# Fused attention kernel: transposes join the score banks, value sums move three groups back, V is loaded whole for the last tile, and the last keys of four heads share a tile

## The reference

```python
scores = jnp.einsum('bthd,bghd->bhtg', Q, K) / np.sqrt(DH)
topv, topi = jax.lax.top_k(scores, K_TOP)            # K_TOP = 32
probs = jax.nn.softmax(topv, axis=-1)
attn = jnp.zeros_like(scores).at[bi, hi, ti, topi].set(probs)
attn_mean = attn.mean(axis=1)                        # over the 4 heads
c_t = jnp.einsum('btg,bgd->btd', attn_mean, V)       # V: 6404 x 128
```

```python
scores = jnp.einsum('bhqd,bhkd->bhqk', q, k) / jnp.sqrt(D)
out = jnp.einsum('bhqk,bhkd->bhqd', jax.nn.softmax(scores, axis=-1), v)
```

## Time and profile before

| | us |
|---|---|
| Median of 3 runs | 2005.47 (2000.84 to 2008.52) |
| The profiled execution | 2001.17, its span 1999.4 |
| First attention, 198 to 862 us of the span | 664 |
| Second attention, 1075 to 1813 | 738 |
| PE, DVE, ACT busy, whole span | 1590.6, 857.4, 1387.5 |

### The profile page before, as it was taken

How to read it: one execution, slowest core, us unless ns; L and a number is a source line. 1 busy time by engine, 2 the same in 40 slices (tenths; PEclk the granted TensorE clock), 3 DMA queues, 4 the chain that set the end, 5 groups by cost and what they waited for, 6 DMA issues and landing times. The chain is left out here.

```text
span 1999.4 us, 22599 instructions
## 1 busy us (share of the span) xinstructions
PE 1590.6 (80%) x8229; PEld 609.5 (30%) x8229; DVE 857.4 (43%) x2286; ACT 1387.5 (69%) x1382; POOL 177.6 (9%) x153
## 2 busy tenths in 40 slices
PE   4357978888788788356464999999999999995996
PEld 3236334445444455333220111111111111113332
DVE  5734699999899898836320000000000000003223
ACT  3471678778778787410224999999999999992432
POOL 2743021111111111100000000000000000000000
PEclk8566989999999999678666999999999999997998
DMA  2122086796786876767002000610070000003000
GB/s 86 51 92 97 11 163 150 165 209 144 172 193 136 196 166 157 167 110 113 21 12 37 1 1 1 56 14 1 7 64 1 1 1 1 1 1 91 0 0 11
DMA packets 91348, 145.08 MB, mean 73 GB/s; under 512 B 46704, under 2 KB 59465, under 8 KB 90433
## 3 DMA queue, kind: packets, MB, share of 16 engines
q0 software_dynamic: 13472, 75.53, 18.9%
q1 hardware_dynamic: 77328, 67.19, 15.7%
q10 hardware_dynamic: 432, 0.85, 0.1%
HBM read 54.15 MB, written 13.99 MB: 34 GB/s over the span
## 5 line engine op out<-in xcount | busy, mean ns | idle before, releaser
L1735 ACT ACTIVATE ex<-ps 128x1536 f32<-128x1536 f32 x544 | 731.2, 1496 | 1.2 <-PE ps L1694 1.0
L1707 PE MATMUL ps<-ex,V 128*9 128x512 f32 x3264 | 427.3, 596 | 0.2 <-ACT ex L1735 0.2
L753 PE MATMUL ps<-K,qst 128*128 128x512 f32 (+1 forms) x832 | 380.3, 601 | 20.6 <-ACT srow L819 14.7
L1694 PE MATMUL ps<-Q,K 52*128 52x512 bf16 x1632 | 328.9, 385 | 64.9 <-ACT ex L1735 33.3
L1745 DVE COPY o<-ps 9x512 f32<-9x512 f32 x32 | 22.0, 687 | 742.8 <-PE ps L1707 742.0
L947 DVE MAX8 cand<-srow 128x8 f32<-128x200 f32 (+1 forms) x1024 | 320.8, 363 | 8.0 <-ACT srow L819 8.0
L819 ACT COPY srow<-ps 128x1024 f32<-128x1024 f32 (+1 forms) x224 | 206.0, 922 | 98.8 <-PE ps L753 98.2
L907 DVE SCALAR_TENSOR_TENSOR both<-srow,top,both 128x1536 f32<-128x1536 f32 (+1 forms) x128 | 240.1, 1876 | 42.5 <-ACT both L835 42.3
L835 ACT ACTIVATE both<-srow,shift 128x1536 f32<-128x1536 f32 (+1 forms) x128 | 209.0, 1636 | 10.5 <-DMA both<-both 9.4
L753 PEld LDWEIGHTS ps<-K,qst 128*128 128x128 f32 x832 | 157.9, 201 | 177.1 <-issue 139.1
L1694 PEld LDWEIGHTS ps<-Q,K 52*128 52x128 bf16 x1632 | 60.2, 94 | 482.0 <-ACT ex L1735 446.8
(11 more groups left out here) (306 smaller groups left out, 1064.0 us busy)
## 6 DMA issues: line engine op xcount, KB each, us to landing
both<-both POOLq DMA_DIRECT2D x69, 768.0 KB, 8.8
v_ring<-v_rows SPq DMA_DIRECT2D x96, 256.0 KB, 3.9
both<-both POOLq DMA_DIRECT2D x23, 898.0 KB, 12.6
K<-k_parts SPq DMA_DIRECT2D x48, 204.0 KB
k_parts<-kl SPq DMA_DIRECT2D x12, 384.0 KB, 2.5
V<-v_rows SPq DMA_DIRECT2D x4, 918.0 KB, 30.8
v_rows<-v1g SPq DMA_DIRECT2D x12, 288.0 KB, 3.0
v_rows<-V SPq DMA_DIRECT2D x12, 256.0 KB, 3.2
```

The source lines that it names most:

```text
L753: last = M.matmul(ps[:, GBANK * (k % RING) + b, 0:c1 - c0], qst[:, h, :], K0[:, c0:c1], start=True, stop=True)
L1694: last = M.matmul(ps[:, n % 6, :], K1[rows_, quad % 2, hh // 2, g * P:(g + 1) * P], Q1[rows_, 4 * quad + hh, tb * TB:(tb + 1) * TB], start ...
L1707: last = M.matmul(ps[32 * j:32 * j + VW, 6 + w % 2, :], V1[:, quad % 2, g, VW * j:VW * j + VW], ex1[:, (4 * g + j) % NSLOT, :], start=g == ...
L1735: C.activation(ex1[:, n % NSLOT:n % NSLOT + NBANK, :], ps[:, n % 6:n % 6 + NBANK, :], ACT.Exp)\
```

## The change

**First attention.** The transposes get no bank of their own. Score groups and transposes are put in one list `ITEMS` in the order in which ACT empties them, and dealt to a ring of 7 banks: two for a group, one for its last part of 260 and for a transpose; where two don't fit at the end, the ring starts again at 0. `BANK_OF` holds the bank, `FREE_AT` the count of `evac` at which its last users are out. ACT's copies of scores and of transposes now both count on `evac`. `meanT` has four slots. The sums of piece j stand three groups behind its transposes (`VALUE_LAG`). PE's order in the head in which a tile's last pieces lie, from the transposes of piece 10 on. Before (L753 scores, L767 transposes, L779 sums):

Before, three units with a sum and one without followed each other here as everywhere, and a unit never had more than three products. The diff, cut to its core:

```diff
-    RING = 3
+    RING = 7
+    MSLOTS = 4
+    VALUE_LAG = 3
+    TAIL_LAG = 3
@@
-            MEAN_AT[first + (SPREAD if u < NT - 2 else HURRIED)[i]] = (u, i)
+            k = first + (SPREAD if u < NT - 2 else HURRIED)[i]
+            TURN_AT[k] = (u, i)
+            VALUE_AT[k + VALUE_LAG] = (u, i)
+        SUMS_AT[k + VALUE_LAG + 1] = u
+    BANK_OF, FREE_AT, at, held = [], [], 0, {}
+    for n, (kind, k) in enumerate(ITEMS):
+        size = min(GBANK, NBK - (k % NGRP) * GBANK) if kind == "scores" else 1
+        if at + size > RING:
+            at = 0
+        BANK_OF.append(at)
+        FREE_AT.append(max(held.get(b, 0) for b in range(at, at + size)))
+        for b in range(at, at + size):
+            held[b] = n + 1
+        at += size
@@ scores
-                    if k >= RING:
-                        pe.wait_ge(S("evac"), k - RING + 1)
+                    if FREE_AT[item]:
+                        pe.wait_ge(S("evac"), FREE_AT[item])
@@ turn_group
-                    if m >= 1:
-                        pe.wait_ge(S("meanT_sb"), m if u < NT - 1 or j == 0 else m - 1)
+                    if u < NT - 1:
+                        pe.wait_ge(S("evac"), FREE_AT[ITEM_AT["turn", (u, j)]])
+                    elif j >= RING:
+                        pe.wait_ge(S("tail_copied"), j - RING + 1)
@@ sync
-                for m in range(NT * NTURN):
+                for m in range(IN_TAIL):
+                    if m == IN_TAIL - 2:
+                        sp.wait_ge(S("kept"), kept_by(LAST - 2, LOW))
+                        sp.dma_start(srow[:, (LAST - 2) % SLOTS, 0:(NG - 1) * P],
+                                     v0_rows[:, 0:NG - 1, :].rearrange("p n d -> p (n d)")).then_inc(S("v0_whole"), 16)
...
+                sp.wait_ge(S("summed"), IN_TAIL)
+                sp.dma_start(v0_ring[:, (NT * NTURN - 1) % 2, (NG - 1) % 4, :], v0_rows[:, NG - 1, :]).then_inc(S("v0_whole"), 16)
@@ load_quad
+        sp.dma_start(V1[:, b, 0:FULL1, :], v1_rows[:, 0:FULL1, quad * 4 * VW:(quad + 1) * 4 * VW]).then_inc(values_in, 16)
+        for j in range(4):
+            h0 = (4 * quad + j) * VW
+            sp.dma_start(V1[LEFT * j:LEFT * (j + 1), b, FULL1, 0:VW], v1_rows[0:LEFT, FULL1, h0:h0 + VW]).then_inc(values_in, 16)
@@ second attention
+        NTILE = 4 * FULL1 + 1
+        NU = NTILE // NBANK
...
+                        for hh in ([n % 4] if g < FULL1 else range(4)):
...
+                                out, col = ps[LEFT * hh:LEFT * (hh + 1), bank(w, n), :], LEFT * hh
+                                keys = slice(g * P, g * P + LEFT)
...
+                            left = slice(LEFT * j, LEFT * (j + 1))
+                            last = M.matmul(out, V1[left, quad % 2, g, 0:VW], ex1[left, slot(w, NTILE - 1), :],
+                                            start=False, stop=True, tile_position=(LEFT * j, 32 * j))
```

More of the change, by code:

```diff
@@ L660, in program @@
     CUTS = [min(4 * P * sum(CH_OF[:c]), G) for c in range(NCH + 1)]
+    LOW = NCH - 1
     LAST = NI - 1
@@ L673, in program @@
         for i in range(NTURN):
-            MEAN_AT[first + (SPREAD if u < NT - 2 else HURRIED)[i]] = (u, i)
-        if u < NT - 2:
-            SUMS_AT[first + SPREAD[-1] + 2] = u
+            k = first + (SPREAD if u < NT - 2 else HURRIED)[i]
+            TURN_AT[k] = (u, i)
+            VALUE_AT[k + VALUE_LAG] = (u, i)
+        SUMS_AT[k + VALUE_LAG + 1] = u
+    ITEMS = []
+    for k in range(NI * NGRP):
+        ITEMS.append(("scores", k))
+        if k in TURN_AT:
+            ITEMS.append(("turn", TURN_AT[k]))
+    ITEM_AT = {item: n for n, item in enumerate(ITEMS)}
+    BANK_OF, FREE_AT, at, held = [], [], 0, {}
[8 more added lines that the diff above has]
+        at += size
     DEEP = 3
@@ L728, in edge_by, with evac_by, v0_tile @@
             return n * STEPS + 8
+        IN_TAIL = (NT - 1) * NTURN
         def turn_bank(m):
-            return 6 if m < (NT - 1) * NTURN else 5 + m % 2
+            return BANK_OF[ITEM_AT["turn", divmod(m, NTURN)]] if m < IN_TAIL else (m - IN_TAIL) % RING
+        def evac_by(k):
+            return ITEM_AT["scores", k] + 1
+        def v0_tile(u, c):
+            if u == NT - 1 and c < NG - 1:
+                return srow[:, (LAST - 2) % SLOTS, c * P:(c + 1) * P]
+            return v0_ring[:, (u * NTURN + c // 4) % 2, c % 4, :]
         def home_free(eng, n, c):
@@ L817, in evac @@
                     act.wait_ge(S("scored"), n * NGRP + g + 1)
-                    b = GBANK * ((n * NGRP + g) % RING)
-                    C.copy(srow[:, n % SLOTS, g0:g1], ps[:, b:b + GBANK, :].rearrange("p a b -> p (a b)")[:, 0:g1 - g0])\
+                    b = BANK_OF[ITEM_AT["scores", n * NGRP + g]]
+                    C.copy(srow[:, n % SLOTS, g0:g1],
+                           ps[:, b:b + -(-(g1 - g0) // 512), :].rearrange("p a b -> p (a b)")[:, 0:g1 - g0])\
                         .then_inc(S("evac"), 1)
@@ L1179, in program @@
     KIN = 12
+    FULL1 = G // P
+    LEFT = 32
+    VIN = 1 + 4
+    assert NG == FULL1 + 1 and G - FULL1 * P <= LEFT
     oq, k1s = ExitStack(), ExitStack()
@@ L1659, in program, with last_tile, group_of, bank @@
         NPASS = NQ * NB
-        NU = 4 * NG // NBANK
-        assert 4 * NG % NSLOT == 0 and NSLOT % NBANK == 0
-        def ready_at(g):
-            return (4 * g + 3) // NBANK + 2
-        def last_key(u):
-            return (NBANK * u + NBANK - 1) // 4
+        NTILE = 4 * FULL1 + 1
+        NU = NTILE // NBANK
+        assert NTILE % NBANK == 0 and NSLOT % NBANK == 0
+        def last_tile(g):
+            return min(4 * g + 3, NTILE - 1)
+        def ready_at(g):
+            return last_tile(g) // NBANK + 2
+        def group_of(tile):
+            w, n = divmod(tile, NTILE)
+            return w * NG + min(n // 4, FULL1)
+        def bank(w, n):
+            return (w * NTILE + n) % (2 * NBANK)
+        def slot(w, n):
+            return (w * NTILE + n) % NSLOT
         with nc.Block() as block:
```

117 lines of the change are left out of this document (64 added, 53 removed).

## The result

| | before | changed |
|---|---|---|
| Median (us) | 2005.4 | 1975.1 (1970.3 to 1984.1) |
| Ratio to before | 1 | 0.986, 95% interval 0.982 to 0.990 |
| The profiled execution's span | 1999.4 | 1982.3 |
| Start to the second end of a selection | 248.9 | 247.8 |
| From there, 29 heads | 559.6 | 535.4 |

The change makes the kernel 1.4% faster; a second set of runs gave a ratio of 0.985 (0.983 to 0.988). The forecast was 1974. The profiled execution was the longest of the changed kernel's four, and its span is only 17.1 us under before's. The table says where: 24.5 us are gained up to the last sum, and 12 are lost where nothing was meant to change.

A forecast was written before the change was run, and what follows sets the result against it. DVE, plus PE's bad moments, was taken to bound the first attention's body, and ACT the second attention. The terms -31.7 + 2.5 - 1.6 = -30.8 us took 2005.5 to 1974.7, given as 1974, range 1955 to 1993.

The forecast's parts named there:

- Body, 29 heads: First attention, second to 31st end of a selection: of 36.1 us lost, 31.7 are gained; bounds 36.1 and 16.
- V's load in the last head: First attention's end: loading V whole for the last tile makes DVE's last head 10.5 us later; bounds 0 and 10.5.
- Tail: First attention, DVE's last add to the last sum: 18.5 us become 8.6; gain 9.9 or about 6, 8 taken.
- Stages between: Loads ahead of the second attention: the four small loads of V per quad lie behind work and cost nothing.
- Second attention: 67 exponentials per pass: 10.8 us less on ACT, 9.2 lost; net gain 1.6, bounds 10.8 and a loss of 5.
- where PE has 12 us of room per tile: First attention: the waits for V's pieces move behind the sixth score group, where PE has 12 us of room per tile.
- The clock's rival: First attention: PE runs ahead in bursts, then stands, and its clock falls; slower, 2027 us; chance 0.05.
- nothing changes: First attention: PE is late for want of banks, so the 36 us stay; 2006 us in all; chance 0.05.
- ACT's copy of those sums ... would be ready first: First attention's end: ACT's copy of the sums behind V's load, ahead of the last head's exponentials, would be ready first.
- three more at 0.53/3: Second attention, pass end: the set has six products, three more at 0.18 us each, so ACT stands 0.5 us.
- The shared bank's rival: Second attention: the last keys' four products, writing one bank, don't overlap; 0.8 us more per pass, 1981 us; chance 0.15.
- the masks still wait in the packed heads: First attention, heads where a tile's last transposes and sums are packed: masks still waiting there was a sign of being wrong.

The follow-up runs named there:

- the square: Sums as before or three groups later, against transposes in their own bank or one ring of 7: old place 1996.8 us, own bank 2010.5, both changed 1975.1.
- the run with pieces: The changed kernel with V for the last tile in pieces of 256 KB as before: 1978.0 us, ratio 0.985.
- the four edits: Changed kernel with x_sb first, small V loads ahead of the large one, transposes two groups apart throughout, shared tile's sum one unit later: 1950.7 us, ratio 0.972.
- V in two loads: The run with the four edits, with V for the last tile in two loads, the second behind the last accumulating transfer: 1945.5 us, ratio 0.969.
- x_sb first: x_sb loaded ahead of keys and values of quads 0 and 1: 1969.7 us, ratio 0.982, in the changed kernel; 1988.4, 0.991, in the kernel before.

## Why the prediction was right, point by point

| step | forecast | measured |
|---|---|---|
| Body, 29 heads | -31.7 | -24.2 and -30.8; means of five profiles of the change and three of before: -24.9 |
| V's load in the last head | +10.5 | +7.3, and 1.2 more behind it |
| Tail | -8 | -7.7 |
| Stages between | 0 | +12.0 and +5.9; +2.4 to +14.4 in the other kernels with x_sb last |
| Second attention | -1.6 | -3.2 |

**Body.** The chain that I followed back in rows 3 and 4 was the right one, and the square shows that both parts of the change are needed for it. The size is too large: 8.6 us are left in the mean where I left 4.4. The step that failed is "where PE has 12 us of room per tile": the room is there over a tile, but the last piece of V is waited for in one group's time, and PE's lead is a group. The clock's rival, and that nothing changes, have no support: the grant stayed 0.93. Stretches at 1.2 GHz remain behind waits for V's pieces (514.45 us) and also behind waits for ACT's copies (PE stood 2.13 us up to 504.52, and the granted clock is 0.50 from 504.8 to 508).

**V whole.** Direction and mechanism as forecast, shown by the run with pieces. The delay was mis-sized by 2 us: I had 10.5, and it came out at 7.3 + 1.2. The accumulating transfer of 898 KB that POOL issues beside the load tells which term was off. The DMA views of its issue, before (801 to 806 us) and changed (778 to 779.5):

```profile
both<-both POOLq DMA_DIRECT2D x1, 898.0 KB, 11.4
```

```profile
srow<-v_rows SPq DMA_DIRECT2D x1, 3200.0 KB, 18.2
both<-both POOLq DMA_DIRECT2D x1, 898.0 KB, 21.1
```

| | lands after (us) | less 11.4 and the room of 2.5 | 31st to 32nd end, less 16.8 |
|---|---|---|---|
| V whole, the changed kernel | 21.1 | 7.2 | 7.3 |
| V whole, with the four edits | 19.3 | 5.4 | 5.5 |
| V in two loads | 16.2 | 2.3 | 2.3 |
| V in pieces | 13.6 | -0.3 | 0 |

So the sum "delay less room" holds to 0.1 us wherever the transfer is late enough, and the term that was mis-sized is the 13.0 us that the load takes from this transfer: 9.7. The other figure that I set beside it, from the page of the Trainium skill (DMA: Bandwidth & Descriptors, Anatomy of one DMA), 9.5 us and a delay of 7.0, lies nearer. That its rate holds here is not shown by that: V's own load took 18.2 us from issue to landing. The 1.2 us are a step that failed: "ACT's copy of those sums ... would be ready first". It came last (807.59 us), and the first mask of the last head waited 2.82 us where it had waited 1.64.

**Tail.** 10.8 us from the last add to the last sum, forecast 8.6 at full clock. Six transposes were left after the last add, not four, since PE had run at the 1.2 GHz level until then (granted clock 0.50 from 803 to 822 us). I had allowed for such a start, and the gain of 8 that I took is what came (7.7).

**Second attention.** The number of exponentials is as counted, 536. A seam costs ACT 0.84 us, not 1.1: 0.69 for the two sums, where I had 0.6, and 0.15 for the last unit's set, where I had 0.5. The step that failed is that set at "three more at 0.53/3", and with it the room of 0.04 us: the small products cost 0.12 each, so the set is 0.32 us longer and not 0.53, and 0.15 of that reaches ACT. The shared bank's rival is out: by it the set takes 1.90 us, and it took 0.85. This also speaks against what I quoted from the Trainium skill (TensorEngine Tiling (Array Packing), Gotcha 1: PSUM Pressure, and Key Properties) for this kernel. The page says that different row tiles can't write one bank at the same time; the four products of two row groups into one bank, each group in partitions of its own, follow each other at 0.12 us, faster than the 0.18 of the large ones, and show no stop. Nor does the change of tile size show: two large, four small and three large ones take 0.36 + 0.49 + 0.53 = 1.38 us.

**Stages between.** I put them at nothing, since the small loads "lie behind work". They did cost nothing, but the stretch took 217.7 to 229.1 us in the seven profiles with V whole in the first attention and x_sb last, and 214.7, 217.1 and 218.8 in the three without that load. I named no risk there, since I had not asked what ends the film stage. It is SP, held behind V's short pieces. Why SP stands 28 to 34 us in the small instructions behind quad 0's V in those seven profiles, and 23 to 26 in the four without V whole, I can't say; with x_sb first it was 26.4, 24.0 and 19.9 with that load. It stays open. The queries' load varies by itself.

**The total.** By the terms the change gives 24.9 - 8.5 + 7.7 + 3.2 = 27.3 us, less what the stages between take, 6.4 us in the mean (223.3 in those seven profiles, 216.9 in the three): 20.9. The medians give 30.3 in both sets of runs (2005.4 to 1975.1, 2003.9 to 1973.5). The profile of before was 4 us under its median, and in which stage the other executions spend those 4 us no profile shows; for the other 5 I have no account either. So 1974 against 1975 is in part luck, from errors of opposite sign: the body 7 us too good and the stages between left out, and against them the last head (2 us), the second attention (1.6) and the 9 us that no term holds. (Among the rivals' sums, "with one of the two, 1957" comes to 1958 with V's load hidden and to 1961 with the seams hidden.)

**The signs that I named.** The masks' waits for exponentials in the body are 9.3 us in the first profile and 3.1 in the second, against 32.8 before; I had left 4.4 (12 with the 7.7 of the start-up). But some of the packed heads still take up to 21.6 us in place of 18.05, and "the masks still wait in the packed heads" was a sign of being wrong: the cause was right and is only in part removed. PE waits for V's pieces at the start of heads, as forecast (514.45 us). ACT waits 6.1 us for the accumulating transfer after head 29, where I had 12.

## What to carry to other kernels

A wait costs by what stands behind it: give the engine a lead first (a shared ring, no wait on the step just before), then move the uncertain wait to where the lead is; apart they gave about 4 us and cost about 9, together they gave 25. Ask of every stage what its last engine does, also of stages that a change doesn't touch: a load issued behind a full queue holds the barrier, and moving one line gave 18 us in the kernel before (and 5 in the changed one, where small loads still stood behind the large one). A large load beside a saturated queue is paid at once by whoever waits for that queue, and half of it could wait here until the queue was empty.

## What the runs showed of the hardware

- A transfer of about 6400 short pieces is issued in 0.4 us, but the next one on the same queue stands 20 to 33 us (25 stands in 14 profiles). SP issues nothing else in that time.
- Four products of 32 x 512 that fill the four quarters of one bank, from two row groups, took 0.12 us each, 0.49 in all, where four of 128 x 512 at 0.18 take 0.71.
- After PE stood 1.91 and 3.14 us for V, the next 12 score products took 8.37 and 7.89 us in place of 5.2. After stands of 1.81 and 3.35 us only the next four were slow, 3.10 and 3.18 us in place of 1.88, and after one of 2.33 us (for ACT) the next four took 1.98. So a late piece of V costs 1.2 to 3.2 us beyond its wait, and a longer wait doesn't mean a longer slow stretch.
- An accumulating transfer of 898 KB landed 11.4 us after its issue in the kernel before, with others of its kind and V's small pieces under way. It took 16.2 with a load of 1.57 MB issued beside it, and 21.1 with one of 3.28 MB, which itself took 18.2 us.
- The load of the queries took 31 to 37 us in profiles of kernels that are the same in that stage. A difference of 5 us between two single profiles says nothing here.
